# Step two's threshold search: a bracket of ten octaves and six halvings in place of sixteen and seven

## The reference

```python
def _top_p_attention(X, W1, W2, W3):
    q = X @ W1.T @ W2.T
    k = X @ W3.T
    probs = softmax(q @ k.T, axis=-1)
    idx = argsort(-probs, axis=-1)
    sp = take_along_axis(probs, idx, axis=-1)
    cs = cumsum(sp, axis=-1)
    mask = zeros.at[rows, idx].set(cs - sp < 0.9)
    A = probs * mask
    return A / maximum(A.sum(-1, keepdims=True), 1e-12)
R = (S + eye) / row sums
for n in range(2):
    A = _top_p_attention(Xa, W1, W2, W3)
    Xf, Xa = R @ Xf, A @ Xa
    Z = Z + Xf @ U1[n].T + Xa @ U2[n].T
```

## Time and profile before

| | us |
|---|---|
| runs: median (lowest to highest of 3) | 2689.44 (2689.21 to 2690.14) |
| the profiled execution, its own time | 2681.91 |
| its span, first to last instruction | 2680.1 |
| step two's pairs in it | 552 to 1418 |
| its mean granted TensorE clock | 0.950 of full speed |

### The profile page before, as it was taken

The page is one execution under the profiler, slowest core; times in us unless marked ns, Lnnn a source line. Parts: engine busy times, 40 slices in busy tenths (PEclk is TensorE's granted clock), DMA queues, the critical chain, the costliest instruction groups (busy, mean ns, idle before and its releaser), DMA issues. The chain is left out here.

```text
span 2680.1 us, 53786 instructions
## 1 busy us (share of the span) xinstructions
PE 2326.0 (87%) x17795; PEld 1967.5 (73%) x17795; DVE 2159.6 (81%) x6687; ACT 1070.0 (40%) x1803; POOL 149.3 (6%) x342
## 2 busy tenths in 40 slices
PE   7999999878899979988976459987999999999995
PEld 2666666657677867767756459876999999999962
DVE  4777777578787888888889677757999999999956
ACT  5666666433334444334422230004344433444333
POOL 0000000111111111000010000000000000000000
PEclk8999999989999989999978769999999999999997
DMA  4000000022223322222212135542343343333320
GB/s 134 2 2 1 1 1 1 2 103 78 81 101 116 116 78 104 103 78 82 105 48 83 63 134 213 206 178 103 105 136 124 120 139 104 131 128 112 121 92 26
DMA packets 57310, 244.88 MB, mean 91 GB/s; under 512 B 6929, under 2 KB 18576, under 8 KB 43344
## 3 DMA queue, kind: packets, MB, share of 16 engines
q1 hardware_dynamic: 57040, 241.99, 25.8%
HBM read 235.15 MB, written 6.82 MB: 90 GB/s over the span
## 5 line engine op out<-in xcount | busy, mean ns | idle before, releaser
L2319 PE MATMUL a_acc<-H,pT 128*128 128x128 f32 x4056 | 547.8, 277 | 11.8 <-ACT a_rows L2352 3.8
L2319 PEld LDWEIGHTS a_acc<-H,pT 128*128 128x128 f32 x4056 | 495.3, 192 | 28.8 <-DVE pT L2455 20.0
L992 PE MATMUL small<-XR,wT 128*128 128x128 f32 x2756 | 379.0, 283 | 26.7 <-ACT wT L1262 26.1
L992 PEld LDWEIGHTS small<-XR,wT 128*128 128x128 f32 x2756 | 344.3, 197 | 42.6 <-ACT wT L1262 42.6
L863 PE MATMUL lg<-kT,qs 128*128 128x512 f32 (+1 forms) x742 | 339.8, 594 | 27.3 <-ACT e L1180 16.8
L73 DVE MAX8 cand<-e 128x8 f32<-128x64 f32 (+3 forms) x1898 | 302.8, 241 | 48.8 <-issue 25.3
L2455 DVE TENSOR_TENSOR pT<-a_tr,a_adjT 128x512 f32<-128x512 f32 (+1 forms) x546 | 316.7, 645 | 20.7 <-PE a_tr L2278 15.6
L2278 PE MATMUL a_tr<-ident,prob 128*128 128x128 f32 x2028 | 311.2, 273 | 10.9 <-ACTq L2346 10.9
L1262 ACT ACTIVATE wT<-tr 128x512 f32<-128x512 f32 (+1 forms) x371 | 206.7, 566 | 276.9 <-PE tr L982 275.9
L892 PE MATMUL accR<-XR,adj 128*128 128x129 f32 x2704 | 312.6, 275 | 0.0
L892 PEld LDWEIGHTS accR<-XR,adj 128*128 128x128 f32 x2704 | 308.5, 192 | 0.0
(11 more groups left out here) (351 smaller groups left out, 2419.8 us busy)
## 6 DMA issues: line engine op xcount, KB each, us to landing
adj<-in_adjT SPq DMA_DIRECT2D x52, 1664.0 KB, 7.2
g_adj<-in_adjT SPq DMA_DIRECT2D x26, 1664.0 KB, 6.8
a_adj<-in_adj SPq DMA_DIRECT2D x26, 1664.0 KB, 7.0
a_adjT<-in_adjT SPq DMA_DIRECT2D x156, 256.0 KB, 3.9
a_adjT<-in_adjT SPq DMA_DIRECT2D x26, 128.0 KB, 4.1
XT<-in_x_t SPq DMA_DIRECT2D x1, 1664.0 KB, 7.2
hT_scratch<-hT SPq DMA_DIRECT2D x1, 1664.0 KB, 11.3
nsT_scratch<-nsT SPq DMA_DIRECT2D x1, 1664.0 KB, 5.3
```

Of the source, the lines that this page charges most:

```text
L992: mm = eng.matmul(accA[:, :], wT[(k * NC + c - 1) % 2][:, o:o + P], xa[:, j, 0:P], start=(j == 0), stop=(j == T - 1))
L2319: mm = eng.matmul(acc[:, :], pT[g % RING][:, (j % 4) * P:(j % 4 + 1) * P], H[:, j, :], start=(j == 0), stop=(j == T - 1))
```

## The change

It gives the search of step two's pairs a bracket and a first step of its own. The bracket goes from 0x3AC00000 (1.5 x 2^-10) up to 1.5, ten octaves (twice five times 2^23), where it went from 0x37C00000 (1.5 x 2^-16) up to the same 1.5, sixteen octaves. The halvings are six instead of seven. The last step is 5 x 2^18 in place of 2^20. The late batch and `another_round` keep `LOW_BITS` and `FIRST_STEP`.

```diff
-HALVINGS = 7
+HALVINGS = 6
+PAIR_LOW_BITS = 0x3AC00000
+PAIR_FIRST_STEP = 5 << 23
...
-    def solve_halving(self, eng, cand, halvings):
+    def solve_halving(self, eng, cand, halvings, low_bits=LOW_BITS, first_step=FIRST_STEP):
...
-        eng.memset(mid, LOW_BITS + FIRST_STEP)
+        eng.memset(mid, low_bits + first_step)
...
-        step = FIRST_STEP
+        step = first_step
         for h in range(halvings):
...
                             find.solve_halving(eng, [find.cand[k][:, 0:SEGS[1], :].rearrange("p a b -> p (a b)")
-                                                     for k in range(2)], HALVINGS)
+                                                     for k in range(2)], HALVINGS,
+                                               low_bits=PAIR_LOW_BITS, first_step=PAIR_FIRST_STEP)
```

## The result

| | before | after |
|---|---|---|
| runs: median (lowest to highest of 5), us | 2689.21 (2683.28 to 2690.14) | 2668.65 (2667.54 to 2673.42) |
| the profiled execution, us | 2681.91 | 2673.42 |
| its span, us | 2680.1 | 2671.6 |

The ratio, which is that of the means, is 0.9935, with a 95% interval from 0.9922 to 0.9947: the means differ by 17.6 us and the medians by 20.6 us, where the forecast was 13.4 us. The time lies in the range (2667 to 2684), near its lower end. The two profiled executions are only 8.5 us apart. These differences need an account. The forecast was made for the whole time, but all its terms lie inside step two, so I hold them against that first. Two single executions of the whole study, 3763.4 us of the changed kernel and 4440.04 us of the kernel before, ran at mean granted clocks of 0.594 and 0.832 and are left out of every interval.

What follows compares the result with a forecast made beforehand. The length of VectorE's own instruction list was taken to set the period in most pairs, with TensorE waiting. The terms 24.3 - 1.9 - 1.7 - 7.3 = 13.4 us gave 2676.0 us, range 2667 to 2684 us.

Steps and rivals of the forecast that it cites:

- The halving that goes: Step two's pair searches: one halving of 1.87 us fewer in each of 13 pairs, 24.3 us of VectorE time gross.
- Pair 0: Start of step two: VectorE's wait for TensorE at the turned flags grows by 1.87 us, so 0 us gained.
- Pairs 1 to 5: TensorE keeps its own pace in pairs 3 to 5; VectorE's lead loses 1.7 us at pair 3's row sums.
- a wait on ScalarE ahead of line 1449: Sign named beforehand: if VectorE showed such waits, the forecast would be wrong; no size given.
- The branches: Spilled rows pass 80 slots one pair sooner; pair 6 gets two more match_replace, 15 instead of 13, costing 7.3 us.
- Pairs 7 to 12: Late pairs of step two: TensorE waits for VectorE again, so their savings of 1.87 us each arrive whole.
- I take them as unchanged: Issue stalls after the loops' ends, up to 6.1 us, assumed the same; one could move the result by up to 6 us.
- To the end of the step: Late batch behind pair 12: one VectorE chain, TensorE waits 13.86 us at its end, so the net gain passes through.
- The sum against the median: Whole time: 13.4 us less, moved from the profiled execution to the median 7.5 us above it, giving 2676.0 us.
- the unmoved switch: Rival, chance 0.12: count stays at 80 or less after pair 5, 13 match_replace remain, gain 20.7 us, 2668.7 us.

Runs made afterwards that it cites:

- after again: The changed kernel measured and profiled once more with no edit: 2669.39 us, ratio 0.9927 to the kernel before.
- the spare halvings: Changed kernel plus one thrown-away halving per search: 2692.56 us in all pairs, 2683.27 us in pairs 0 to 6 alone, 2681.49 us in pairs 7 to 12 alone.

## Why the prediction came out as it did

Starts of searches divide step two into stretches (552.34, 616.11, 944.52 and 1009.36 in before; 551.18, 614.42, 937.42 and 1007.85 in after; 550.47, 614.14, 935.01 and 1005.45 in after again); the last one ends with the last selection. In the second profile of before these stretches are within 0.3 us of the first.

| stretch | forecast | after | after again |
|---|---|---|---|
| pair 0 | 0 | -0.5 | -0.1 |
| pairs 1 to 5 | -7.6 | -5.4 | -7.5 |
| pair 6 | +5.4 | +5.6 | +5.6 |
| pair 7 to the last selection | -11.2 | -13.0 | -14.0 |
| sum, us | -13.4 | -13.3 | -16.0 |

- **The halving that goes** (24.3 us gross): right in count and in size; the spare halvings show that it is worth its time in early and late pairs alike; in pair 0 one run shows it free, the other doesn't.
- **Pair 0**: right. The wait for the turned flags took up the saving, 2.24 to 3.85 us.
- **Pairs 1 to 5**: right in kind. TensorE holds its own pace in pairs 3 and 4 (63.0 and 62.1 us in all profiles but one, where it is 63.25 and 62.06), and VectorE runs into it once, in pair 3. The place was wrong: I saw the 0.1 us of slack at the row sums, and the main stop came ahead of the next pair's maxima. It is called issue; in the program the wait for ScalarE's last exponentials stands there, and these ended at 772.3, the maxima beginning at 772.35 (770.0 and 770.01 in the other profile), so I read it as the wait for them. It cost 3.0 and 0.4 us in one profile, 1.0 and 0.4 us in the other, against 1.7 us forecast. Of the 3.0 us, and of the 2.1 us by which the two columns differ, 1.4 is TensorE's lower clock in pair 2 and not the change. I had also named a wait on ScalarE ahead of line 1449 as a sign against the forecast; it shows, with 0.8 us in 3 places (0.3 us in 1 before), and weighs nothing. Without any stop the sum of step two would be 15.1 us, which lies between the two profiles as well: the rows show the stop, the time doesn't.
- **The branches**: right to the pair, in six kernels (13, 15, 13, 11, 15 and 11 match_replace). Counting what the data does was the step that decided most: without it, the two match_replace would be missing from the sum, and six halvings in sixteen octaves would have looked as good as the changed kernel, while they are 445 us slower than before.
- **Pairs 7 to 12**: right in kind, mis-sized by 2 to 3 us. The step that failed is "I take them as unchanged", said of the issue stalls. In these pairs and the late batch they fell from 28 to 26 us in sum, those ahead of the match_replace from 8.6 to 2.7 and others rising; that is about 2 of the 2 to 3 us. The runs with 20 and 40 memsets show such pieces changing when nothing but the place of the instructions does. That the shorter search acted here by moving what lies behind it fits, and isn't shown by itself.
- **To the end of the step**: right, the 13.86 us ahead of the last transpose stayed to the hundredth.
- **The sum against the median**: the rest of the 20.6 us is not all accounted for. The first search starts 1.2 us earlier, in work that the change doesn't touch; over all kernels it starts between 550.5 and 552.3. What remains lies behind the last selection: 3.9 us of spread ahead of the next stage, and up to 7.5 us in that stage from one profile to the next. The median executions of before were longer than its profiled ones, by 7.5 us at first; I moved the forecast by that amount as if it were a constant, and after the change it had the other sign (the profiled execution lies 4.8 us above the median). That the sum in step two agrees (13.3 us in one profile, 16.0 in the other) is no luck in its terms, but the 13.3 is: the dip in the clock hid some 1.4 us of gain and the late pairs gave 1.8 us too much. That the median lies in the range hangs in part on executions that nobody profiled. No long execution of before was profiled, so where it spends the excess is open.

Of the rivals, the unmoved switch came nearest in time (2668.7 us) and is wrong by its mechanism: line 458 stands at 15. The time alone would have confirmed it.

## What to carry to other kernels

Where a change alters the precision of a search, count on the data which rows then take another branch; the number of one rare instruction (13, 15, 11) then bears out where the branch falls, while the time can't. When two engines are level, price a saving on one of them by going through the stretches and asking where the other stops it and where the lead is cashed in. And compare executions at a point inside the program ahead of a stage that varies by itself, with two profiles of each kernel: even that point moved by 3.4 us.

## What was not expected

Forty instructions of nothing, put where VectorE was idle, brought the last selection of step two 7 to 11 us forward (1485.9 against 1493.1 and 1496.5), and 20 did not (1497.4). And what is left of a nest of three hardware loops after its work is done cost 15.8 to 17.4 us of idle VectorE for each tile, over a third of the 42.0 us of a round.
